# Routing of the first two batch rows moved among attention's raw products, in a two-layer gated block kernel

## What is computed

```
x = x + tanh(g_xattn[0]) * attention0(layernorm(x), ctx)      # biased, time bias, output projection
x = x + tanh(g_ffn[0])   * ffn0(layernorm(x))                 # ternary weights, relu, 256 -> 1024 -> 256
x = x + tanh(g_xattn[1]) * attention1(layernorm(x), ctx)      # relu on q, k, v, no output projection
x = x + tanh(g_ffn[1])   * experts1(layernorm(x))
```

```
logits = x @ W_router                       # (tokens, 4)
expert_idx = argmax(logits)
h = gelu(x @ W1[expert] + b1[expert])       # 256 -> 1024, erf form
y = layer_norm(h @ Wo + bo + x) * gamma + beta
```

## Time and profile before

| | us |
|---|---|
| median of three runs | 829.76 |
| the profiled execution | 835.91 |
| its span | 834.1 |
| TensorE busy | 737.3 (88%) |
| VectorE busy | 581.4 (70%) |
| ScalarE busy | 440.8 (53%) |
| GpSimd busy | 296.2 (36%) |
| second attention's group 14 starts its scores at | 602.86 |
| its last transposes end at | 648.07 |
| first block of the experts starts at | 653.59 |

### The profile page before, as it was taken

The page is one execution under the profiler, slowest core; times in us unless marked ns, Lnnn a source line. Parts: engine busy times, 40 slices in busy tenths (PEclk is TensorE's granted clock), DMA queues, the critical chain, the costliest instruction groups (busy, mean ns, idle before and its releaser), DMA issues.

```text
span 834.1 us, 12041 instructions
## 1 busy us (share of the span) xinstructions
PE 737.3 (88%) x4096; PEld 428.6 (51%) x4096; DVE 581.4 (70%) x1126; ACT 440.8 (53%) x840; POOL 296.2 (36%) x348
## 2 busy tenths in 40 slices
PE   5897599999998998999768999899999886899991
PEld 3443234343432676777523334333353775799981
DVE  5473689999970489265758899799943537577775
ACT  2222488888887535665016888687853422233330
POOL 2121255555554234755000000755423304233322
PEclk9897699999999999999877999999975989899996
DMA  8497355454444431002722255522012202111100
GB/s 298 112 180 219 108 179 180 169 170 155 166 166 155 152 101 51 1 1 73 173 62 81 71 175 169 149 77 64 18 46 83 92 1 90 39 48 44 42 15 21
DMA packets 51357, 87.52 MB, mean 105 GB/s; under 512 B 8598, under 2 KB 16792, under 8 KB 51297
## 3 DMA queue, kind: packets, MB, share of 16 engines
q1 hardware_dynamic: 44320, 72.06, 28.2%
q0 software_dynamic: 4576, 11.54, 5.3%
q10 hardware_dynamic: 2400, 3.15, 1.1%
HBM read 45.29 MB, written 41.63 MB: 104 GB/s over the span
## 4 chain that ended last, share of the span: by engine, by line
PE 56%; issue 11%; DVE 11%; DMA 8%; POOL 6%; SPq 4%; ACT 3%; POOLq 0%; DVEq 0%; ACTq 0%
PE ps_out L712 14%; PE ps_a L698 10%; PE ps_wide L593 6%; DVE row_max L1395 5%; PE ps_misc L698 5%; PE ps_a L522 4%; DMA out_x<-sorted_rows,ids 3%; PE ps_a L830 3%; SPq L438 2%; PE ps_wide L688 2%; POOL sorted_rows L1287 2%; PE ps_wide L894 1%; POOL hid_lo L1255 1%; PE ps_out L844 1%; ACT probs L1020 1%
## 5 line engine op out<-in xcount | busy, mean ns | idle before, releaser
L1395 DVE TENSOR_REDUCE row_max<-ps_wide 128x2 f32<-128x1024 f32 x256 | 301.1, 1219 | 34.0 <-PE ps_wide L593 27.8
L1020 ACT ACTIVATE probs<-ps_a 128x512 f32<-128x512 f32 x342 | 191.5, 602 | 57.4 <-PE ps_a L698 49.4
L593 PE MATMUL ps_wide<-stack_k,stack_q 48*128 48x512 f32 x512 | 155.1, 472 | 15.2 <-DVE row_max L1395 11.0
L698 PE MATMUL ps_a<-stack_q,stack_k 62*128 62x512 f32 (+1 forms) x342 | 142.3, 467 | 13.1 <-ACT probs L1020 10.1
L712 PE MATMUL ps_out<-probs,vals 128*17 128x512 f32 x1024 | 142.2, 631 | 0.5 <-POOL probs L1214 0.5
L698 PEld LDWEIGHTS ps_a<-stack_q,stack_k 62*128 62x128 f32 (+1 forms) x342 | 61.9, 194 | 102.4 <-ACT probs L1020 69.3
L1020 ACT ACTIVATE probs<-ps_misc 128x512 f32<-128x512 f32 x170 | 102.4, 603 | 19.4 <-PE ps_misc L698 15.5
L1214 POOL TENSOR_TENSOR probs<-probs,fixes_sb 128x512 f32<-128x512 f32 x64 | 82.2, 1284 | 82.5 <-ACT probs L1020 82.5
L593 PEld LDWEIGHTS ps_wide<-stack_k,stack_q 48*128 48x128 f32 x512 | 63.0, 191 | 50.5 <-DVE row_max L1395 20.2
L698 PE MATMUL ps_misc<-stack_q,stack_k 62*128 62x512 f32 (+1 forms) x170 | 78.8, 463 | 2.9 <-ACT probs L1020 2.9
L1199 POOL TENSOR_SCALAR max_neg<-row_max 128x16 f32<-128x16 f32 x32 | 9.2, 289 | 158.5 <-DVE row_max L1395 137.3
(11 more groups left out here) (214 smaller groups left out, 1326.7 us busy)
## 6 DMA issues: line engine op xcount, KB each, us to landing
rows_sorted<-blank SPq DMA_DIRECT2D x17, 1040.0 KB, 5.0
planes_k<-planes SPq DMA_DIRECT2D x32, 256.0 KB, 3.8
planes_q<-planes SPq DMA_DIRECT2D x32, 256.0 KB, 3.5
stack_q<-planes_q SPq DMA_DIRECT2D x64, 128.0 KB, 2.8
stack_k<-planes_k SPq DMA_DIRECT2D x64, 128.0 KB, 2.8
w_raw<-in_L_W SPq DMA_DIRECT2D x6, 1024.0 KB, 5.1
stack_q<-planes_q SPq DMA_DIRECT2D x64, 64.0 KB, 2.7
stack_k<-planes_k SPq DMA_DIRECT2D x64, 64.0 KB, 2.6
```

What stands on the lines that cost most here:

```text
L593: mm(raw_slot(l, ("pair", g, p))[:, i * S:(i + 1) * S], stack_q[at, slot(g, c) + q * P:slot(g, c) + (q + 1) * P], stack_k[at, slot(g, c):s ...
L698: mm(score_slot(("tile", n))[:], stack_k[at, slot(g, c) + k * P:slot(g, c) + (k + 1) * P], stack_q[at, slot(g, c):slot(g, c) + S], start=T ...
L1020: do(probs[n % PROBS[l]][:, j, :], score_slot(("tile", n * HG + j))[:], ACT.Exp, scale=0.25).then_inc(exp_done, 1)
L1395: v.tensor_reduce(row_max[:, g % 2, :, p], raw_slot(l, ("pair", g, p))[:].rearrange("p (i k) -> p i k", i=2), AX, ALU.max).then_inc(sem(f" ...
```

## The change

Routing of batch rows 0 and 1 leaves groups 14 and 15. TensorE transposes row 0 in its group 11 and makes its logits at the end of it, counts in group 12; row 1 is transposed and has its logits in group 13 and is counted in group 14. VectorE normalises row 0 at the end of its loop for group 12, routes at the end of that for 13, and so on. GpSimd scatters row 0 before it makes the high part of the second weights. Two of the gather buffers are now such that both lie in slots of group 13, so that blocks 0 and 1 can be gathered when group 13's scores are done. In the expert phase logits(2), count(2), turn_n3(3), logits(3), place(3) and tables(1) each come later by up to a block, the first low halves come ahead of row 3's updates, and GpSimd's loop becomes root4(n), scatter(n - 3), gather(n + 4).

The diff, cut to what matters for the order of work:

```diff
+                if len(w_mo_hi) == 2:
+                    sorted_rows.insert(1, sorted_rows.pop(ROW_RING - 3))
...
         def raw_items(l):
             for g in range(G + BEHIND + 2):
-                if l == 1 and g == G + 1:
-                    for what, b in (("n3", 0), ("n3", 1), ("logits", 0), ("count", 0), ("logits", 1), ("count", 1)):
-                        yield (what, b)
+                if l == 1 and g == G - 2:
+                    yield ("logits", 0)
+                if l == 1 and g == G:
+                    yield ("logits", 1)
+                    yield ("count", 1)
                 for p in range(PAIRS):
+                    if l == 1 and (g, p) in ((G - 3, 6), (G - 1, 6)):
+                        yield ("n3", (g - G + 3) // 2)
+                    if l == 1 and (g, p) == (G - 2, 2):
+                        yield ("count", 0)
...
                             scores(g, k, c, 1)
-                            if l == 1 and (g, k, c) == (G - 2, 2, 0):
-                                turn_n3(1)
-                        if l == 1 and (g, k) == (G - 2, 2):
-                            route_logits(0)
-                        if l == 1 and (g, k) == (G - 2, 3):
+                        weigh(g * QT + k - BEHIND)
+                        if l == 1 and (g, k) in ((G - 5, 2), (G - 3, 2)):
+                            turn_n3((g - G + 5) // 2)
+                        if l == 1 and (g, k) in ((G - 5, 3), (G - 3, 3)):
+                            route_logits((g - G + 5) // 2)
+                        if l == 1 and (g, k) == (G - 4, 0):
                             count(0)
-                            route_logits(1)
-                        weigh(g * QT + k - BEHIND)
-                        if l == 1 and (g, k) == (G - 1, 0):
+                        if l == 1 and (g, k) == (G - 2, 0):
                             count(1)
                             total(0)
...
-                        if l == 1 and (g, k) == (G - 2, 1):
-                            turn_n3(0)
...
+            turn_rows(0)
             turn_n3(2)
-            route_logits(2)
-            turn_rows(0)
...
                 if n == 0:
+                    route_logits(2)
+                if n == 1:
                     count(2)
                     turn_n3(3)
-                if n == 1:
+                if n == 2:
                     route_logits(3)
                 if n > 0:
                     down(n - 1)
                 turn_hidden(n)
-                if n == 1:
+                if n == 2:
                     count(3)
                     total(1)
...                                                   # ScalarE
-                            if l == 1 and j == 0 and g == G - 2 and k - 2 in range(EARLY_ROWS):
-                                if k == 2:
-                                    act.wait_ge(sem("b1_split"), 1)
-                                rows1(k - 2)
+                            if l == 1 and (g, k, j) == (G - 5, 3, 0):
+                                act.wait_ge(sem("b1_split"), 1)
+                                rows1(0)
+                            if l == 1 and (g, k, j) == (G - 3, 3, 0):
+                                rows1(1)
...                                                   # GpSimd
+                    if l == 1 and g == G - 4:
+                        roots(3, 1)
                     if l == 1 and g == G - 3:
+                        pool.wait_ge(sem("rows_cleared"), 16 * (G + 1))
+                        number_rows()
+                        place_rows(0)
                         hidden_weights()
...
-                if n == 0:
-                    pool.wait_ge(sem("scores_done1"), QT * B * H)
+                if n in (0, 2):
+                    pool.wait_ge(sem("scores_done1"), QT * HG * (G - 2 if n == 0 else G))
...
-            roots(3, 1)
-            pool.wait_ge(sem("rows_cleared"), 16 * (G + 1))
-            place_rows(0)
             place_rows(1)
             roots(3, 2)
-            for n in range(2):
+            for n in range(FIRST):
                 gather(n)
             roots(3, 3)
-            for n in range(2, FIRST):
+            place_rows(2)
+            root4(0)
+            root4(1)
+            place_rows(3)
+            root4(2)
+            for n in range(FIRST, FIRST + 2):
                 gather(n)
-            place_rows(2)
-            place_rows(3)
-            for n in range(3):
-                gather(FIRST + n)
-            for n in range(2):
+            for n in range(3, BLOCKS):
                 root4(n)
-            for n in range(2, BLOCKS + 2):
-                if n < BLOCKS:
-                    root4(n)
-                scatter(n - 2)
-                m = n + ROW_RING - 2
-                if FIRST + 3 <= m < BLOCKS:
-                    gather(m)
+                scatter(n - 3)
+                if n + 4 < BLOCKS:
+                    gather(n + 4)
+            for n in range(BLOCKS - 3, BLOCKS):
+                scatter(n)
...                                                   # VectorE, attention
+                        if l == 1 and (g, p) == (G - 2, 2):
+                            place(0)
                         if g < G:
                             maximum(l, g, p)
-                    if l == 1 and g >= GB + BEHIND + 2:
+                    if l == 1 and GB + BEHIND + 2 <= g < G - 4:
                         update3(g - GB - BEHIND - 2)
-                        if g % GB == GB - 1:
-                            aggregate(3, (g - GB - BEHIND - 2) // GB, 1e-5)
+                    if l == 1 and g == G - 5:
+                        aggregate(3, 0, 1e-5)
+                    if l == 1 and g == G - 4:
+                        update3(4)
+                        update3(5)
+                        normal(3, 0, x)
+                    if l == 1 and g == G - 3:
+                        route(0)
+                        update3(6)
+                        update3(7)
+                        aggregate(3, 1, 1e-5)
+                    if l == 1 and g == G - 2:
+                        normal(3, 1, x)
+                    if l == 1 and g == G - 1:
+                        route(1)
...                                                   # VectorE, expert phase
+            rows_low(0)
             for t in tiles(3, None):
                 update3(t)
             aggregate(3, 3, 1e-5)
+            rows_low(1)
             route(2)
-            rows_low(0)
             normal(3, 3, x)
-            rows_low(1)
-            place(2)
             hidden_low(0)
             for n in range(1, BLOCKS + 1):
+                if n == 3:
+                    place(3)
+                    tables(1)
                 if n + 1 < BLOCKS and n != FIRST - 1:
                     rows_low(n + 1)
+                if n == 1:
+                    place(2)
...
+                if n == 2:
+                    route(3)
                 if n < BLOCKS:
                     hidden_low(n)
-                if n == 1:
-                    route(3)
-                if n == 2:
-                    place(3)
-                    tables(1)
                 if n == 3:
                     finish(0)
-                if n > 2 and n < BLOCKS:
+                if n == 4:
+                    finish(1)
+                if 4 <= n < BLOCKS:
                     finish(n - 2)
                 spread(n - 1)
```

More of the change, by code:

```diff
@@ L1165, in expert_weights, with number_rows, place_rows @@
                 halves(w1_hi[:, e, cols], w1_lo[:, e, cols], w1_raw1[:, e, cols], QT * e + q)
+            def number_rows():
+                pool.wait_ge(sem("w_last"), 16 * 7)
+                v.tensor_copy(rows_all[:, :, 2 * D:ROW], table[:, TOKENS:STEPS].unsqueeze(2).broadcast_to([P, T, ROW - 2 * D])
+                              ).then_inc(sem("numbered"), 1)
+                pool.wait_ge(sem("numbered"), 1)
+            def place_rows(b):
+                pool.wait_ge(sem("dest_ready"), b + 1)
+                for t in range(b * QT, (b + 1) * QT):
+                    nc.gpsimd.indirect_dma_start(rows_sorted, bass.IndirectOffsetOnAxis(dest[:, t:t + 1], 0), rows_all[:, t, :], None
+                                                 ).then_inc(sem("rows_sent"), 16)
             def hidden_weights():
```

22 lines of the change are left out of this document (4 added, 18 removed).

## The result

Over 17 runs each, on the same chips in turn, the changed kernel took 841.34 us as its median and the kernel before 831.56. The ratio is 1.0098, 95% interval 1.0067 to 1.0128: slower by 8.1 us (5.6 to 10.6), where the two medians are 9.8 apart. The forecast was +7.0. The profiled execution of the changed kernel took 837.87 us, 3.5 under its median; that of the kernel before was 4.4 over its own. So the pair of profiles shows only 2.0 us of the difference in span (836.1 for 834.1), and 2.05 of opposite sign lie before anything that was changed: group 12's maxima start at 557.37 for 559.42.

A forecast was written before the change was run, and what follows sets the result against it. TensorE and VectorE together pace attention's groups and TensorE the expert phase, apart from holes and low clock. Terms 16.1 - 3.8 - 7.3 + 1.5 + 0.5 = +7.0 us gave a median of 836.8, range 819 to 842.

The forecast's parts named there:

- VectorE has no slack: Attention's groups 10 to 13: VectorE, busy 10.7 of 11.19 us, has half a microsecond of slack; these groups cost +16.1.
- The second rival: Attention: the maxima's schedule has room, so added work costs 8 instead of 16.1 us; total -1.1, 828.7; chance 0.2.
- The low clock in groups 10 to 13: Attention: low clock behind two holes of TensorE costs 1.2 and 1.5 us, +2.7 together, between 0 and 6.
- The reason I gave for the fall: Groups 10 to 13: holes in TensorE's work bring its clock down, as behind 3.01 us of standing before group 10.
- Groups 14 and 15: Attention's last groups: clock falls 1 to 4 us into group 14 and stays down; 41.4 us for 45.2, -3.8.
- first rival: Groups 14 and 15: the clock holds or comes back, -18.7 us there; total -7.9, 821.9, faster; chance 0.3.
- the forecast's case: Groups 14 and 15: clock falls and stays down, 41.4 us; forecast total +7.0, chance 0.5 with the third rival.
- Stays down, as it did: Groups 14 and 15: after falling, the clock stays at 1.2 GHz to the last weighted sums, a quarter taking 4.04 us.
- The expert phase: Behind attention: up(0) to up(6) takes 60.4 us for 66.0; with the earlier start -7.3, between -3 and -12.
- The third rival: Expert phase: its holes stay where they are, -3 instead of -7.3 us; 841, counted within the forecast's chance of 0.5.
- The wait on gathers: Expert phase from block 7: every gather late by about 0.5 us, 0.2 a block; +1.5 over ten blocks, 0 to 3.
- The tail: End of kernel: one more scatter stands behind the last root, +0.5 us (0 to 1.3).

The follow-up runs named there:

- the kernels with one half each: Changed kernel with the old expert phase: 847.06 us, ratio 1.0173 to before; kernel before with the changed expert phase alone: 828.21 us, ratio 0.9945.
- whole-array repeats: Changed kernel with 128-row products repeated ahead of normal(3, 0)'s hole and behind logits(1) and count(1) with total(0): 840.65 us, ratio to before 1.0117.
- narrow products: Changed kernel with a 50-row score product repeated ten times ahead of normal(3, 0)'s hole and ten ahead of the wait for route(0): 850.82 us, ratio to before 1.0113.
- The run with normal(3, 0) alone: Kernel before with only VectorE's share in group 12 moved (two updates and normal(3, 0) behind its maxima): 836.11 us, ratio to before 1.0013.

## Why the prediction was right, and where not

The sign and the size were right: +7.0 forecast, +8.1 measured (5.6 to 10.6). By halves I had +12.3 for attention and -5.3 for what is behind it; the kernels with one half each measured +14.4 (11.3 to 17.6) and -4.6 (-6.7 to -2.4). That the total came within 1.1 us is in part luck: inside attention two terms were off by more than the sum shows, in opposite directions (in the pair of profiles +21.3 for +16.1, and -13.6 for -3.8).

- **VectorE has no slack** held. Group 12 cost +2.9 for my +3.0, the hole was 2.39 for 3.0, the wait for logits(0) 1.51 for 1.5. The second rival, that the schedule has room, fell: its 8 us were 21.3.
- **The low clock in groups 10 to 13** was the mis-sized term: 2.7 us, bounded by 6. The maxima for group 14 came 21.0 us after those for 13, not 17, and of this 4.0 go when the clock holds (16.94 then). The two stretches behind took 8.6 more than before for my 7.3, with half clock again around count(0). I priced the fall by the group 10 of the earlier trace rows, where VectorE lost 0.98 and the clock was back within 4 us. In group 13 it stood at half for some ten us, with the normalisation's transposes and the eight of row 0 in them (1.95 us for 1.04), but not logits(0). Group 10 itself varies: behind the same hole the changed kernel's profile has ten us at half clock, and VectorE waits 1.68 and 1.71 more. One group of one execution was too little to price it by.
- **The reason I gave for the fall**, that a hole of TensorE brings it, did not hold as put. The fall does come with the move of normal(3, 0): it was there in all eight profiles that keep it at the end of group 12 and have no whole-array repeats, and one of these has nothing else moved. In seven of them the hole is there too. But the eighth, with TensorE busy in the hole by narrow products, has the same fall, and with whole-array products in the same place it did not come. That rests on one profiled execution for each filling.
- **Groups 14 and 15** came between forecast and first rival. The clock fell within them as forecast, and then came back after 13.8 us: 31.64 for 41.4. Of the seven profiles with the moved routing and no repeats in these groups, four took 31.1 to 31.7 us and three 38.8 to 40.8, so the forecast's case exists too, and these few don't show which is the usual one. "Stays down, as it did" was taken over from a stretch with twice the small products; whether that is the difference, no run shows.
- **The expert phase** held: up(0) to up(6) 59.4 for 60.4, -7.6 for -7.3 from the end of attention. Up(0) came only 1.0 us earlier behind the last transposes for my 1.7. The hole before row 3's counts became 0.82 for about 1.0; block 5's rows came 2.70 late for 2.4, its low half 2.17 more, 4.9 in all where I had some 3.8 left of the hole. The third rival, that these holes stay, fell.
- **The wait on gathers** is real and was priced at half: 3.2 us for 1.5, just over my upper bound of 3. Each chain was as worked out (6.2 us from residual to root, the gather 8.3 behind the residual), and late by 0.5. A late block shifts the next ones, so only every second or third waits; but such a wait cost 0.7 to 0.87 us of the pitch, where I counted only its own length.
- **The tail** was +0.7 for +0.5.

**What stays open.** The run with normal(3, 0) alone took 7.3 us more than before from group 12's maxima to the end in its profile and 1.1 in its timed runs. Either most executions escape the fall, or the kernel before loses something there too in executions that no profile shows. The granted clocks of the timed runs fit both: their mean is 0.925 over twelve executions of this kernel and 0.925 over the 23 of the kernel before beside them. Also open is why the clock comes back in groups 14 and 15 in some executions of the same code and not in others.

## What to carry to other kernels

Work that is moved onto an engine without slack pays its own time and may take TensorE's clock with it: price the clock by the instructions of that stretch at half speed (4.0 us here), not by what another hole cost in one execution (1.2). Time the halves of a change by themselves: here one was +14 us and the other -5, and two small orders inside the good half, a gather ahead of a root that waits and a small consumer ahead of long finishing work, were worth some 10 us more.

## What was not expected of the hardware

- With TensorE busy for 2.46 of 2.46 us, on 50-row products for the most part, the granted clock fell to 0.50 behind them; with 2.45 of 2.45 us, on 128-row products for the most part, it stayed at 1.00 for the next 9.65 us (one profiled execution of each). The Trainium skill (TensorE: Matmul & The Clock Gate, What's actually happening) says that the clock is set by how busy the PE has been. By busy time as these rows count it the trace does not agree: it was the same in both, and in the stretch of 55.46 us above TensorE was busy for 53.22 at a mean clock of 0.63. What the grant follows beyond that, no run here shows.
- An update with two operands in SBUF took 1.27 us for 0.47 while GpSimd ran a two-operand instruction, and ended 0.3 after it (555.47 + 1.27 for 555.18 + 1.28). The Trainium skill (SBUF — State Buffer, SBUF: two separate sides) says that these two engines share a port pair, as a lock held for the whole instruction; the trace agrees. The maxima, which read PSUM, kept their 1.2 us there.
- The same attention code took 31.6 us in its last two groups in three profiled executions and 38.8 in a fourth.
